# A graph network on one core: where the fourth quarter of the edge distances is made, and how often groups of VectorE instructions signal

## The chip, the cores and the metric

The kernel runs on one core of a Trainium2 chip. The metric is the device time of one execution in microseconds (us). TensorE (PE) multiplies matrices, VectorE (DVE) does elementwise work, reductions and scans, ScalarE (ACT) evaluates functions, GpSimd (POOL) issues the indirect transfers, and SyncE (SP) the others. The engines run their own instruction streams and wait for each other by semaphores.

## What is computed

A graph has 12,500 nodes of 64 features and 212,500 edges. Four layers follow one another, each added to its input and normalised. Cut to what matters (`seg` sums the rows of one node):

```python
# layer 0, twice:  out = D_inv * seg(e[edge_idx], node_idx);  e = B_inv * seg(xt[node_idx], edge_idx)
# layer 1:         softmax of edge_attr_64 @ W_fcr.T over each dst, applied to (h[src] + eh)
# layer 2, similarity:
Wr, Wc = Wh[row], Wh[col]
sim = sum(Wr * Wc) / maximum(|Wr| * |Wc|, EPS)
prop = seg((base * relu(+-sim))[:, None] * Wc, row)
# layer 3:
d = gelu(layer_norm(edge_attr_3 @ Wd1 + bd1, g1, b1))
d = gelu(layer_norm(d @ Wd2 + bd2, g2, b2))            # the edge distances
logits = w1[dst] - w2[src] + d
a = softmax of logits over each dst
out = seg(a * (w3[src] + d), dst)
```

The distances `d` need only the edge attributes, not the nodes, so they may be made in any earlier stage. They are used in the last one.

## The kernel before, in words

**Tiling.** The edges are padded to 128 x 1664: each of the 128 partitions holds 1664 edges in a row (`NT`). A pass takes `T` = 64 columns of edges at a time, so it has 26 chunks (`NCH`) of 8192 edges. The softmax passes take 52 columns and have 32 chunks.

**A pass over the edges.** The helper `gathers` issues 64 indirect transfers per chunk from POOL (L923), one for each column, which fetch a row of a node table for every edge into `rows[b]`, b = 0 or 1. When a chunk is there, DVE runs one `tensor_tensor_scan` for each of the 64 features over the chunk's columns, which makes the running sums of each node, and copies the last column as the start of the next chunk. SP loads the indices `idx` of a chunk and stores its sums.

**The stages**, in order: `sum_pass("conv0d")`, `sort_edges`, `moved_pass`, `sum_pass("conv1d")`, `sum_pass("conv1s")`, `softmax_pass("L1")`, `similarity_pass`, `softmax_pass("L3")`, with small phases between them. The first sum stage over sums is meant by conv1d, the second by conv1s. Each is a block of its own; engines meet between blocks.

**The distances** are made by the class `Distances` in parts of 16 columns. A part is two halves. For half 0, PE transposes the attributes (L981) and multiplies (L986), ACT copies and squares (L1015, L1017), DVE reduces and scales (L1046, L1047), ACT takes the root, DVE divides and applies gain and offset (L1050, L1051, L1054 twice), and ACT applies Gelu. Half 1 does the same on Gelu's result, after PE's transposes and multiplications (L997, L1002, L1004) and ACT's copies (L1024, L1026). There is one buffer `Y`, so the parts follow one another. SP loads the attributes (L971) and stores the part, 512 KB (L976). 26 parts are a quarter of all. conv0d makes quarter 0, conv1d quarter 1, both with one part in each chunk (`per` = 1), and conv1s makes quarters 2 and 3 with two parts in each chunk (`per` = 2).

In a chunk of a sum stage DVE does half 0 of the first part, the 64 scans, the copy, half 1, and with `per` = 2 then both halves of the second part. In conv1d the sums are also multiplied by a share (`mean`, L1235). SP's order is that of `load`, `step` and `store` at L1150 to L1175: load the indices of chunk n, store chunk n-1 (sums and distances), load those of chunk n+1, and so on. POOL starts a chunk's gathers when its indices are there and the store of the sums two chunks back has landed.

**The similarity stage** has no distances, and PE and ACT do nothing in it. In a chunk DVE runs 65 scans over `own` (L2029: the row of the edge's own node, spread over its edges), a copy (L2031), then a chain of eleven instructions (L2041 to L2051) that computes the similarity and multiplies the gathered rows, and 64 scans over the result `tmp` (L2054) with a copy (L2056). The end of L2051 is the signal `msg`; POOL starts the gathers of a chunk when `msg` of the chunk two before has come.

Every one of these scans adds one to a semaphore, and the instruction behind the group waits for the full count:

```python
                    for f in range(F):
                        dve.tensor_tensor_scan(rows[b][:, :, f], k, rows[b][:, :, f], last[:, f:f + 1],
                                               ALU.mult, ALU.add).then_inc(scanned, 1)
                    dve.wait_ge(scanned, (ch + 1) * F)
```

`keep_p` holds, for each edge, whether its node goes on from the column before. In the sum stages it lies as 16-bit numbers in the PSUM tile `held`, in the similarity stage as f32 in a PSUM tile of its own.

Of the kernel before, what the change touches and what calls it, by code (L numbers as in the profile page):

```python
# [32 lines left out]
def gnn_resnorm(nc, x_in, src_0, dst_0, attr3_0, attr64_0, w_0, w2_0, W, out):  # L33
# [239 lines left out]
    class Counting:  # L273
# [38 lines left out]
        def dve(self, dve, i, b):  # L312
            for k in range(T // KC):
# [3 lines left out]
                for d, oh in self.oh[k % 2].items():  # L317
# [3 lines left out]
                    dve.tensor_tensor(oh[:, :, :], v, u, ALU.is_equal).then_inc(self.ready, 1)  # L321
# [6 lines left out]
        def pe(self, pe, i, b):  # L328
            for k in range(T // KC):
                n = (i * 2 + b) * (T // KC) + k  # L330
                pe.wait_ge(self.ready, (n + 1) * 4)
# [124 lines left out]
    def sort_edges(first_row, key, second, third, fill=False):  # L456
# [13 lines left out]
        with ExitStack() as c, nc.Block() as block:  # L470
# [145 lines left out]
            def _(dve):  # L616
# [6 lines left out]
                def digits(i, b):  # L623
                    ch = i * 2 + b
                    dve.wait_ge(loaded[b], (i + 1) * 48)
                    if not zero(i):
                        dve.wait_ge(ohr, ch * 2 * NGP - 2 * NGP)
# [7 lines left out]
                def onehots(ch, b, g):  # L635
                    for src, dst, w in ((lo[b], ohl, P), (hi[b], ohh, HI)):
                        v = src[:, 4 * g:4 * g + 4].unsqueeze(2).to_broadcast([P, 4, w])
                        u = iota[:, 0:w].unsqueeze(1).to_broadcast([P, 4, w])
                        dve.tensor_tensor(dst[b][:, 4 * g:4 * g + 4, :], v, u, ALU.is_equal).then_inc(ohr, 1)
# [47 lines left out]
                def fill_part(i, b, g):  # L687
# [8 lines left out]
                    if g >= GF:  # L696
                        n = NGP - GF
                        for f in range((F + 1) * (g - GF) // n, (F + 1) * (g - GF + 1) // n):
                            v = ec[:, ::-1] if f == F else recs[b][:, ::-1, f]
                            dve.tensor_tensor_scan(recs[b][:, ::-1, f], nxp[:, ::-1], v, after[:, f:f + 1],  # L700
                                                   ALU.mult, ALU.add).then_inc(tail, 1)
                    if g == NGP - 1:
                        dve.wait_ge(tail, (ch + 1) * (F + 1))
# [20 lines left out]
            def _(pe):  # L724
# [4 lines left out]
                def turn(ch, g, b):  # L729
                    if not (zero(ch) and g < 2):  # L730
                        pe.wait_ge(tev, ch * NGP + g - 1)
                    pe.wait_ge(ohr, (ch * NGP + g + 1) * 2)
# [390 lines left out]
    def sum_pass(name, o, idx_arr, table, to, last, first, per, mean=False, hist=None, beside=()):  # L1123
# [6 lines left out]
        with ExitStack() as c, nc.Block() as block:  # L1130
# [18 lines left out]
            def _(sp):  # L1149
# [16 lines left out]
                def store(i, b):  # L1166
# [5 lines left out]
                    else:  # L1172
                        sp.wait_ge(scanned, (i * 2 + b + 1) * F)
# [39 lines left out]
            def _(dve):  # L1213
# [3 lines left out]
                def scan(i, b):  # L1217
# [37 lines left out]
    def moved_pass(last):  # L1255
# [11 lines left out]
        with ExitStack() as c, nc.Block() as block:  # L1267
# [71 lines left out]
            def _(dve):  # L1339
# [3 lines left out]
                for n in range(NM):  # L1343
# [17 lines left out]
                    for f in range(F):  # L1361
                        dve.tensor_tensor_scan(rows[b][:, 0:w, f], kc, rows[b][:, 0:w, f], last[:, f:f + 1],
                                               ALU.mult, ALU.add).then_inc(scanned, 1)
                    dve.wait_ge(scanned, (n + 1) * F)
# [23 lines left out]
    def softmax_pass(name, idx_arr, table, last, lastmax):  # L1388
# [16 lines left out]
        with ExitStack() as c, nc.Block() as block:  # L1405
# [21 lines left out]
            def _(sp):  # L1427
# [29 lines left out]
                def store(ch):  # L1457
                    sp.wait_ge(maxed, ch + 1)
                    sp.dma_start(cols(maxes, ch, TS), Hh[:, 0:TS, :]).then_inc(mstored, 16)
                    sp.wait_ge(summed, (ch + 1) * 2 * F)  # L1460
# [46 lines left out]
            def _(act):  # L1507
# [9 lines left out]
                def fades(i, b):  # L1517
                    ch = i * 2 + b
                    act.wait_ge(dk, ch + 1)
                    if not (isinstance(i, int) and i == 0 and b == 0):  # L1520
                        act.wait_ge(summed, ch * 2 * F)
# [34 lines left out]
            def _(dve):  # L1556
# [3 lines left out]
                def step(i, b):  # L1560
# [19 lines left out]
                    for f in range(F):  # L1580
                        dve.tensor_tensor_scan(Hh[:, 1:TS + 1, f], l[:, :, f], k, Hh[:, 0, f:f + 1],  # L1581
                                               ALU.max, ALU.add).then_inc(hs, 1)
                    dve.wait_ge(hs, (ch + 1) * F)
# [636 lines left out]
```

## Time and profile before

| | us |
|---|---|
| median of 3 runs (lowest, highest) | 24007.1 (23978.64, 24059.23) |
| the profiled execution | 24218.6 |
| its span | 24216.7 |
| DVE busy | 11770.1 (49%) |
| POOL busy | 11836.6 (49%) |
| PE, ACT busy | 4210.8 (17%), 3105.3 (13%) |
| conv1d, from its first gather to its last | 2463 |
| conv1s, the same | 3150 |
| similarity, the same | 2701 |

The profile takes one execution; busy times are sums over all instructions of an engine, and the stages' times are stretches of the span. POOL and DVE are each busy for half of the span, PE and ACT much less. No engine is near its full time, so the order in which engines wait for one another in a chunk has to be read from the trace. The granted TensorE clock was 0.551 of full speed on average.

### The profile page before, as it was taken

How to read it: one execution, taken by the hardware profiler on the slowest of the kernel's cores; microseconds unless marked ns; L12 is line 12 of the kernel's file. 1: busy time of each engine (PE TensorE's matmuls, PEld its weight loads, DVE VectorE, ACT ScalarE, POOL GpSimd, SP SyncE). 2: the span in 40 equal slices, each digit the busy share in tenths (PEclk: the TensorE clock that was granted, in tenths of full speed). 3: DMA queues.
4: the chain of work that ended last, by engine and by line, in shares of the span. 5: the costliest groups of instructions: out<-in, count | busy, mean ns of one | idle time of the engine just before them, and what ended most of it. 6: DMA issues, size and time to landing. Idle time of an engine off the chain costs nothing. (4 is left out here: it accounts for less than half of the span.)

```text
span 24216.7 us, 113497 instructions
## 1 busy us (share of the span) xinstructions
PE 4210.8 (17%) x22758; PEld 3202.0 (13%) x22758; DVE 11770.1 (49%) x32045; ACT 3105.3 (13%) x3839; POOL 11836.6 (49%) x12292
## 2 busy tenths in 40 slices
PE   1222224444440111112222211111100000000000
PEld 1111123333330100001111111111100000000000
DVE  4544554444446233333333346666644454566666
ACT  0101111111110111112222211111100000111111
POOL 5444434333332666654444455555465555545444
PEclk7555557666665555555555555555555555555555
DMA  2111111111114111111111122222222221222222
GB/s 60 38 34 39 38 49 44 44 44 44 44 40 204 41 52 49 52 45 43 43 44 40 44 69 83 84 83 85 76 59 55 63 62 54 89 96 98 99 97 83
DMA packets 546330, 1518.63 MB, mean 63 GB/s; under 512 B 263864, under 2 KB 264397, under 8 KB 494082
## 3 DMA queue, kind: packets, MB, share of 16 engines
q1 hardware_dynamic: 151550, 1028.87, 11.1%
q0 software_dynamic: 392160, 467.91, 9.5%
q10 hardware_dynamic: 2068, 16.12, 0.2%
q14 instruction: 404, 3.31, 0.0%
q8 instruction: 148, 2.42, 0.0%
HBM read 714.46 MB, written 803.57 MB: 63 GB/s over the span
## 5 line engine op out<-in xcount | busy, mean ns | idle before, releaser
L923 POOL DMA_INDIRECT rows<-tab,idx x6656 | 6420.4, 965 | 5273.0 <-issue 2073.0
L571 POOL DMA_INDIRECT moved_rows<-recs,sidx x1664 | 1623.4, 976 | 2362.4 <-DVE sidx L685 1863.6
L1226 DVE TENSOR_TENSOR_SCAN rows<-held,last,rows 128x64 f32<-128x64 f32 (+1 forms) x4992 | 1421.4, 337 | 2055.6 <-issue 1902.7
L923 POOL DMA_INDIRECT rows<-in_x,idx x1664 | 1591.8, 957 | 1691.0 <-DMA idx<-src_d 1191.2
L923 POOL DMA_INDIRECT rows<-sums,idx x1664 | 1573.8, 946 | 1580.1 <-DMA idx<-sedge 1080.3
L1609 DVE TENSOR_TENSOR_SCAN DN<-XB,last,VB 128x52 f32<-128x52 f32 x4096 | 1062.1, 313 | 1261.8 <-issue 1261.4
L1609 DVE TENSOR_TENSOR_SCAN DN<-XB,last,PB 128x52 f32<-128x52 f32 x4096 | 957.4, 307 | 555.4 <-issue 432.7
L2029 DVE TENSOR_TENSOR_SCAN own<-keep_p,lastu,own 128x64 f32<-128x64 f32 x1690 | 543.9, 345 | 1198.7 <-issue 1188.3
L654 DVE CUSTOM_DVE_ANT_0 junk<-pV,ohh 128x98 f32<-128x98 f32 x1664 | 425.5, 256 | 1377.2 <-remote 1137.5
L321 DVE TENSOR_TENSOR oh_dl<-dig_dl,held 128x2048 bf16<-128x2048 uint16 (+1 forms) x104 | 237.7, 2286 | 1485.5 <-remote 1143.0
L986 PE MATMUL dist_ps<-dist_w,a3T 65*128 65x512 f32 x416 | 392.8, 1100 | 3259.8 <-ACT a3T L1010 2347.3
L1581 DVE TENSOR_TENSOR_SCAN H<-logits,H,neg_d 128x52 f32<-128x52 f32 x4096 | 901.5, 304 | 84.9 <-issue 84.9
L1046 DVE TENSOR_REDUCE held<-SQ 128x16 f32<-128x1024 f32 x208 | 254.9, 1225 | 1221.2 <-ACT SQ L1017 769.5
L646 DVE TENSOR_TENSOR same<-pE,mask 128x384 bf16<-128x384 f32 x832 | 440.9, 554 | 770.8 <-remote 509.3
L755 PE MATMUL pV<-place,ohT 128*128 128x98 f32 x1664 | 389.8, 320 | 1947.8 <-issue 927.2
L1485 PE MATMUL pt<-ident,side 128*128 128x128 f32 x832 | 219.8, 412 | 2713.6 <-issue 1491.9
L743 PE MATMUL pE<-ohT 128*128 128x256 f32 x1664 | 633.7, 468 | 229.4 <-issue 179.7
L335 PE MATMUL H_d<-oh_dl,oh_dh 128*98 128x128 bf16 x1664 | 387.7, 305 | 1490.7 <-issue 1013.7
L1640 PE MATMUL pT<-ident,lastmax 128*64 128x128 f32 x2 | 0.8, 393 | 3536.5 <-PEq L62 3536.5
L608 ACT ACTIVATE place<-pP 128x98 f32<-128x98 f32 x832 | 210.7, 253 | 3000.9 <-remote 1354.4
L986 PEld LDWEIGHTS dist_ps<-dist_w,a3T 65*128 65x128 f32 x416 | 122.2, 324 | 3402.1 <-issue 3334.2
L755 PEld LDWEIGHTS pV<-place,ohT 128*128 128x128 f32 x1664 | 284.4, 214 | 2036.2 <-issue 1603.5
(416 smaller groups left out, 16622.0 us busy)
## 6 DMA issues: line engine op xcount, KB each, us to landing
sums<-DN SPq DMA_DIRECT2D x64, 3328.0 KB
sums<-rows SPq DMA_DIRECT2D x52, 2048.0 KB
rows<-tab,idx POOLq DMA_INDIRECT x6656
maxes<-H SPq DMA_DIRECT2D x64, 1664.0 KB
spread<-zeros SPq DMA_DIRECT2D x52, 1040.0 KB
own<-spread SPq DMA_DIRECT2D x26, 2080.0 KB
dists<-Y SPq DMA_DIRECT2D x104, 512.0 KB
recs<-sums SPq DMA_DIRECT2D x26, 2048.0 KB, 16.2
```

Source lines behind the costliest of these rows:

```text
L335: last = pe.matmul(self.H[o][0:HI, :], oh[o + "h"][:, t, :], oh[o + "l"][:, t, :], start=False, stop=False, skip_group_check=True)
L571: pool.indirect_dma_start(moved_rows if fill else rec, bass.IndirectOffsetOnAxis(ap=idx[b][:, j:j + 1], axis=0), recs[b][:, j, :], None).t ...
L646: dve.tensor_tensor(same[g % 2][h][:, :, :], pE[h][:, :, :], mask[:, :, :], ALU.mult).then_inc(msk, 1)
L654: dve.tensor_tensor_reduce(out=junk[:, :], in0=pV[h][:, k, 0:HI], in1=ohh[b][:, t, :], scale=1.0, scalar=0.0, op0=ALU.mult, op1=ALU.add, a ...
L743: pe.matmul(pE[h][:, 0:2, :].rearrange("p a e -> p (a e)"), o[:, 2 * h, :], o[:, 2 * h:2 * h + 2, :].rearrange("p a e -> p (a e)"), start= ...
L755: pe.matmul(pV[h][:, 0, 0:HI], o[:, 2 * h, :], place[:, :], start=True, stop=False)
L923: pool.indirect_dma_start(rows[b][:, j, :], None, table, bass.IndirectOffsetOnAxis(ap=idx[b][:, j:j + 1], axis=0)).then_inc(rows_in[b], 16)
L986: t = pe.matmul(self.p1[:, 8 * h:8 * h + 8, :].rearrange("p a f -> p (a f)"), self.a3T[:, :], dist_w[:, h * 512:(h + 1) * 512], start=True ...
L1226: dve.tensor_tensor_scan(rows[b][:, :, f], k, rows[b][:, :, f], last[:, f:f + 1], ALU.mult, ALU.add).then_inc(scanned, 1)
L1581: dve.tensor_tensor_scan(Hh[:, 1:TS + 1, f], l[:, :, f], k, Hh[:, 0, f:f + 1], ALU.max, ALU.add).then_inc(hs, 1)
L1609: dve.tensor_tensor_scan(DN[:, :, s_ * F + f], XB[:, :, f], a[:, f, :], last[:, s_ * F + f:s_ * F + f + 1], ALU.mult, ALU.add).then_inc(su ...
L2029: dve.tensor_tensor_scan(u[:, :, f], k, u[:, :, f], lastu[:, f:f + 1], ALU.mult, ALU.add).then_inc(filled, 1)
```

## The change

1. conv1s is called with `per` = 1 in place of 2, so it makes only quarter 2.
2. Quarter 3 is made in `similarity_pass`: it gets a `Distances` with one part in each chunk, an instruction stream for PE and one for ACT, half 0 ahead of DVE's step and half 1 behind it, and the load and store on SP. To make room, `keep_p` becomes 16-bit numbers in the tile `held`, and the small tile `a` moves into it too.
3. Groups signal once: in a group of scans, and in the groups that make one-hot masks, only the last instruction adds to the semaphore, and the waits' counts are divided accordingly. That takes out about 23,600 signals: 4914 in the three sum stages, 882 in `moved_pass`, 8128 and 4032 in the softmax passes (L1609, L1581), 3302 in the similarity stage, 1664 in `sort_edges`, and some 700 of the one-hot masks.

The diff, cut to its core (the groups that are not shown are changed in the same way):

```diff
@@ sum_pass, SP and DVE
-                        sp.wait_ge(scanned, (i * 2 + b + 1) * F)
+                        sp.wait_ge(scanned, i * 2 + b + 1)
...
                     for f in range(F):
-                        dve.tensor_tensor_scan(rows[b][:, :, f], k, rows[b][:, :, f], last[:, f:f + 1],
-                                               ALU.mult, ALU.add).then_inc(scanned, 1)
-                    dve.wait_ge(scanned, (ch + 1) * F)
+                        t = dve.tensor_tensor_scan(rows[b][:, :, f], k, rows[b][:, :, f], last[:, f:f + 1],
+                                                   ALU.mult, ALU.add)
+                    t.then_inc(scanned, 1)
+                    dve.wait_ge(scanned, ch + 1)
@@ similarity_pass
-            a, keep_p, keep_in = ps(c, "a", [P, T]), ps(c, "keep_p", [P, NT]), sem("L2_keep_in")
+            held, pa, gains = ps(c, "held", [P, 1024], I32), ps(c, "pa", [P, P]), ps(c, "gains", [P, 4, F])
+            keep_p, keep_b, keep_in = held[:, 0:NT // 2].bitcast(U16), alloc(c, "keep_b", [P, NT], U16), sem("L2_keep_in")
+            a, ss = held[:, 896:896 + T].bitcast(F32), held[:, 960:960 + DW].bitcast(F32)
+            dist = Distances(c, "L2", 3, 1, pa, gains, ss)
@@ similarity_pass, SP
                     sp.dma_start(base[b][:, :], cols(sbase, ch)).then_inc(side_in[b], 16)
+                    dist.load(sp, i, b, 0)
                     if not isinstance(i, int) or i or b:
-                        store(ch - 1)
-
-                def store(ch):
-                    sp.wait_ge(scanned, (ch + 1) * F)
+                        store(*((i - 1, 1) if b == 0 else (i, 0)))
+
+                def store(i, b):
+                    ch = i * 2 + b
+                    sp.wait_ge(scanned, ch + 1)
                     sp.dma_start(cols(sums_s[0:EP, :], ch), tmp[:, :, :]).then_inc(stored, 16)
+                    dist.store(sp, i, b, 0)
@@ similarity_pass, PE and ACT
+            @block.tensor
+            def _(pe):
+                def step(i, b):
+                    dist.pe_first(pe, i, b, 0)
+                    dist.pe_second(pe, i, b, 0)
+                pairs(pe, step)
+
+            @block.scalar
+            def _(act):
+                pairs(act, lambda i, b: dist.act(act, i, b, 0))
@@ similarity_pass, DVE
                     k = keep_p[:, bass.ds(ch * T, T)]
+                    dist.dve(dve, i, b, 0, 0)
                     dve.wait_ge(side_in[b], (i + 1) * 32)
...
                     dve.tensor_copy(last[:, :], tmp[:, T - 1, :]).then_inc(carried, 1)
+                    dist.dve(dve, i, b, 0, 1)
@@ the calls
-        sum_pass("conv1s", "s", sedge, sums, sums_s, last, 2, 2)
+        sum_pass("conv1s", "s", sedge, sums, sums_s, last, 2, 1)
```

**SP in the loop of conv1s**, the piece ahead of the load of a chunk's indices. Before, two parts are stored and two loads of attributes lie around them:

```order
L976 DMA dists<-Y 128x1024
L1173 ISA
L1174 ISA
L1174 DMA sums_s<-rows_614 128x4096
L975 ISA
L976 ISA
L976 DMA dists<-Y 128x1024
L969 REGISTER_ALU
L971 ISA
L971 DMA a_634<-attr_d 128x48
L1153 ISA
L1153 DMA idx_612<-sedge 128x64
```

The same piece now, with the line numbers of the changed kernel:

```order
L1177 DMA sums_s<-rows_614 128x4096
L978 ISA
L979 ISA
L979 DMA dists<-Y 128x1024
L1156 ISA
L1156 DMA idx_612<-sedge 128x64
```

The indices are now loaded behind one store of distances where there were two.

**DVE in the similarity stage**, between the scans over `tmp` of one chunk and those over `own` of the next. Before:

```order
L2054 SCALAR_TENSOR_TENSOR tmp<-keep_p,last,tmp 128x64 x64
L2056 COPY last<-tmp 128x64
L2029 SCALAR_TENSOR_TENSOR own_827<-keep_p,lastu,own_827 128x64 x65
L2031 COPY lastu<-own_827 128x65
L2041 TENSOR_TENSOR tmp<-own_827,rows_825 128x4096
```

Now:

```order
L2087 COPY last<-tmp 128x64
L1049 TENSOR_REDUCE held<-SQ 128x16
L1050 TENSOR_SCALAR held<-held 128x16
L1053 RECIPROCAL held<-held 128x16
L1054 TENSOR_TENSOR Y<-Y,held 128x1024
L1057 TENSOR_TENSOR Y<-Y,gains 128x1024 x2
L1049 TENSOR_REDUCE held<-SQ 128x16
L1050 TENSOR_SCALAR held<-held 128x16
L1053 RECIPROCAL held<-held 128x16
L1054 TENSOR_TENSOR Y<-Y,held 128x1024
L1057 TENSOR_TENSOR Y<-Y,gains 128x1024 x2
L2058 SCALAR_TENSOR_TENSOR own_827<-held,lastu,own_827 128x64 x65
```

Half 1 of one part and half 0 of the next now stand between the two groups of scans.

**SP in the loop of the similarity stage**, one step. Before:

```order
L1981 ISA
L1982 ISA
L1982 DMA idx_822<-sdst 128x64
L1990 ISA
L1990 DMA own_827<-spread 128x4160
L1991 DMA base_829<-sbase 128x64
L1997 ISA
L1997 DMA sums_s<-tmp 128x4096
```

Now:

```order
L1992 DMA idx_822<-sdst 128x64
L2000 ISA
L2000 DMA own_827<-spread 128x4160
L2001 DMA base_829<-sbase 128x64
L974 ISA
L974 DMA a_856<-attr_d 128x48
L2009 ISA
L2009 DMA sums_s<-tmp 128x4096
L978 ISA
L979 ISA
L979 DMA dists<-Y 128x1024
```

A load of attributes (24 KB) now stands ahead of the store of the sums, and a store of distances (512 KB) behind it.

## Rows read from the trace of the kernel before

**Rows 1.** Windows conv1d, conv1s, similarity: us, busy (x) PE PEld DVE ACT POOL, clock.

```profile
8024.00:10487.00 2463.00, 354.07 (x827) 183.05 (x828) 884.97 (x1977) 331.96 (x401) 1573.75 (x1664) 0.51 0.19 49
10541.00:13691.00 3150.00, 683.05 (x1618) 351.31 (x1618) 1008.43 (x2210) 650.38 (x781) 1573.76 (x1664) 0.51 0.16 42
17638.00:20339.00 2701.00, 0.00 (x0) 0.00 (x0) 1287.33 (x3472) 0.00 (x0) 1578.04 (x1664) 0.50 0.23 60
```

**Rows 2.** Timeline of a chunk of conv1s: start us, us, instruction, idle before.

```profile
12110.72 0.94 POOL L923 DMA_INDIRECT rows<-sums,idx  x1 [41.85 <-DMA idx<-sedge]
...
12122.89 7.12 DVE L1226 TENSOR_TENSOR_SCAN rows<-held,last,rows 128x64 f32<-128x64 f32 x29 [0.45 <-issue]
...
12186.52 0.21 DVE L1229 COPY last<-rows 128x64 f32<-128x64 f32 x1 [8.08 <-DMA moved_rows<-dist_w]
...
12196.31 1.22 DVE L1054 TENSOR_TENSOR Y<-Y,gains 128x1024 f32<-128x1024 f32 x1 [0.18 <-DVE Y L1054]
...
12198.85 0.36 SPq L976 DMA_DIRECT2D dists<-Y  x1
...
12205.01 1.23 DVE L1046 TENSOR_REDUCE held<-SQ 128x16 f32<-128x1024 f32 x1 [7.48 <-ACT SQ L1017]
...
12223.36 1.23 DVE L1046 TENSOR_REDUCE held<-SQ 128x16 f32<-128x1024 f32 x1 [12.58 <-ACT SQ L1029]
...
12226.65 2.47 DVE L1054 TENSOR_TENSOR Y<-Y,gains 128x1024 f32<-128x1024 f32 x2
...
12231.95 0.36 SPq L1153 DMA_DIRECT2D idx<-sedge  x1
...
12234.54 0.95 POOL L923 DMA_INDIRECT rows<-sums,idx  x1 [44.08 <-DMA idx<-sedge]
```

**Rows 3.** Timeline of a chunk of conv1d, from the end of its scans.

```profile
9133.30 0.32 DVE L1229 COPY last<-rows 128x64 f32<-128x64 f32 x1 [8.79 <-DMA moved_rows<-dist_w]
...
9137.58 4.42 DVE L1235 TENSOR_TENSOR rows<-rows,held 128x4096 f32<-128x4096 f32 x1 [3.83 <-issue]
...
9156.12 0.95 POOL L923 DMA_INDIRECT rows<-tab,idx  x1 [7.51 <-issue]
```

**Rows 4.** Timeline of a chunk of the similarity stage, DVE and POOL.

```profile
18024.64 15.58 DVE L2054 TENSOR_TENSOR_SCAN tmp<-keep_p,last,tmp 128x64 f32<-128x64 f32 x64
18025.49 0.95 POOL L923 DMA_INDIRECT rows<-tab,idx  x1 [25.84 <-DVE tmp L2051]
...
18040.25 0.20 DVE L2056 COPY last<-tmp 128x64 f32<-128x64 f32 x1
...
18040.58 4.46 DVE L2029 TENSOR_TENSOR_SCAN own<-keep_p,lastu,own 128x64 f32<-128x64 f32 x18
...
18062.88 0.35 DVE L2029 TENSOR_TENSOR_SCAN own<-keep_p,lastu,own 128x64 f32<-128x64 f32 x1 [1.06 <-issue]
...
18113.99 0.20 DVE L2031 COPY lastu<-own 128x65 f32<-128x65 f32 x1 [5.97 <-remote]
...
18130.77 0.95 POOL L923 DMA_INDIRECT rows<-tab,idx  x1 [25.53 <-DVE tmp L2051]
```

**Rows 5.** Timeline of PE in conv0d while a gather ran; these matmuls signal nothing.

```profile
1613.41 0.26 PE L335 MATMUL H_d<-oh_dl,oh_dh 128*98 128x128 bf16 x1 [2.53 <-issue]
1616.21 0.27 PE L335 MATMUL H_s<-oh_sl,oh_sh 128*98 128x128 bf16 x1 [2.54 <-issue]
```

**Rows 6.** Timeline of L1's softmax pass at a gather's end, then DVE's scans.

```profile
15616.94 0.95 POOL L923 DMA_INDIRECT rows<-tab,idx  x1 [0.30 <-issue]
...
15624.63 0.76 DVE L1609 TENSOR_TENSOR_SCAN DN<-XB,last,VB 128x52 f32<-128x52 f32 x3 [0.37 <-issue]
15625.31 5.95 DVE L1609 TENSOR_TENSOR_SCAN DN<-XB,last,PB 128x52 f32<-128x52 f32 x27
```

**Rows 7.** Timeline of conv1s: a hand-over from PE to ACT while a gather runs.

```profile
12147.17 2.08 PE L1004 MATMUL dist_ps<-bd_d,yT 128*128 128x128 f32 x8
...
12172.52 0.60 ACT L1026 ACTIVATE Y<-dist_ps 128x512 f32<-128x512 f32 x1 [27.41 <-DMA klast<-dst_d]
```

**Rows 8.** Costliest groups, the page's part 5: busy, mean ns | idle before.

```profile
L1581 DVE TENSOR_TENSOR_SCAN H<-logits,H,neg_d 128x52 f32<-128x52 f32 x4096 | 901.5, 304 | 84.9 <-issue 84.9
```

More of the change, by code:

```diff
@@ L330, in pe @@
                 n = (i * 2 + b) * (T // KC) + k
[L331 removed]
+                pe.wait_ge(self.ready, n + 1)
                 for t in range(KC):
@@ L699, in fill_part @@
                             v = ec[:, ::-1] if f == F else recs[b][:, ::-1, f]
-                            dve.tensor_tensor_scan(recs[b][:, ::-1, f], nxp[:, ::-1], v, after[:, f:f + 1],
-                                                   ALU.mult, ALU.add).then_inc(tail, 1)
+                            t = dve.tensor_tensor_scan(recs[b][:, ::-1, f], nxp[:, ::-1], v, after[:, f:f + 1],
+                                                       ALU.mult, ALU.add)
                     if g == NGP - 1:
-                        dve.wait_ge(tail, (ch + 1) * (F + 1))
+                        t.then_inc(tail, 1)
+                        dve.wait_ge(tail, ch + 1)
                         dve.tensor_copy(after[:, :], recs[b][:, 0, 0:F + 1]).then_inc(kept, 1)
@@ L1361, in _ @@
                     for f in range(F):
-                        dve.tensor_tensor_scan(rows[b][:, 0:w, f], kc, rows[b][:, 0:w, f], last[:, f:f + 1],
-                                               ALU.mult, ALU.add).then_inc(scanned, 1)
-                    dve.wait_ge(scanned, (n + 1) * F)
+                        t = dve.tensor_tensor_scan(rows[b][:, 0:w, f], kc, rows[b][:, 0:w, f], last[:, f:f + 1],
+                                                   ALU.mult, ALU.add)
+                    t.then_inc(scanned, 1)
+                    dve.wait_ge(scanned, n + 1)
                     dve.tensor_copy(last[:, 0:F], rows[b][:, w - 1, 0:F]).then_inc(carried, 1)
@@ L2005, in _ @@
                 step(NCH // 2 - 1, 1, last=True)
-                store(NCH - 1)
+                store(NCH // 2 - 1, 1)
                 sp.wait_ge(stored, NCH * 16)
+                sp.wait_ge(dist.stored, NCH * 16)
             @block.gpsimd
@@ L2011, in _ @@
                 gathers(pool, tab65, idx, rows, idx_in, rows_in, lambda e, i, b: e.wait_ge(msg, i * 2 + b - 1), go, T, NCH)
+            @block.tensor
[7 more added lines that the diff above has]
+                pairs(act, lambda i, b: dist.act(act, i, b, 0))
             @block.vector
             def _(dve):
+                dist.start(dve)
                 dve.memset(last[:, :], 0.0).then_inc(carried, 1)
                 dve.memset(lastu[:, :], 0.0).then_inc(carried, 1)
-                dve.tensor_copy(keep_p[:, :], keep["s"][:, :]).then_inc(keep_in, 1)
+                dve.tensor_copy(keep_b[:, :], keep["s"][:, :]).then_inc(keep_in, 1)
                 dve.wait_ge(keep_in, 1)
+                dve.tensor_copy(held[:, 0:NT // 2], keep_b[:, :].bitcast(I32)).then_inc(keep_in, 1)
+                dve.wait_ge(keep_in, 2)
                 NS = 10
```

51 lines of the change are left out of this document (29 added, 22 removed).

## The prediction, written before the changed kernel was timed

> **What bounds the kernel now.** The page's busy shares name no engine, so I went by stage. The windows give, for the same 1664 gathers of POOL, 2463 us in conv1d, 3150 in conv1s and 2701 in the similarity stage [rows 1]. POOL is busy for 1574 in each, and with the 0.30 between two gathers [rows 6] it could do a stage in 1574 + 1664 x 0.30 = 2073. All that is above this is POOL waiting, once a chunk. The timelines show for what.
>
> In conv1s a chunk goes from 12110.72 to 12234.54, 123.8 us. DVE's copy after the scans is at 12186.52, half 1 of the first part ends at 12197.53, then the second part waits 7.48 and 12.58 for ACT and ends at 12229.12. Only then come the indices, and POOL has stood idle for 44.08 [rows 2]. So conv1s is bound by DVE's chain, with the second part bare at its end.
>
> In the similarity stage a chunk goes from 18025.49 to 18130.77, 105.3. POOL issues for 79.8 and waits 25.53 for L2051 [rows 4]. The scans over `tmp` run beside the gathers' start, 64 in 15.58. Of the scans over `own`, 18 go quickly (4.46), and then one takes 0.35 with 1.06 idle ahead of it, 1.4 in all, until the gathers are over. Their copy comes at 18113.99, 8.75 after POOL's last transfer and 88.5 into the chunk. L2041 to L2051 take the last 16.8. So DVE, slowed while POOL gathers, bounds this stage.
>
> **The slowing is the point to understand.** After the gathers' end it is gone: in L1 POOL's last gather begins at 15616.94, and from 15625.31 on 27 scans take 5.95 [rows 6]. Is it the scans' signals? PE in conv0d has matmuls that signal nothing, and beside a gather they too start 2.80 apart, with 2.53 idle ahead of each, 1.40 for each of matmul and weight load [rows 5]. So what is slowed is every instruction's end, with or without a signal. Hand-overs are late as well: PE's L1004 ended at 12149.25, and ACT began L1026 at 12172.52, 23.3 later [rows 7].
>
> **Part 1, conv1s with one part.** Removed in each chunk are both halves of the second part and their two waits: 12229.12 - 12197.53 = 31.6 on the path, as the indices are then loaded behind the first part's store (it was issued at 12198.85) and not the second's. Times 26 this is **-821**, and the stage takes 2329. The nearest stage with one part is conv1d. As it stands it takes 2463, which gives -687. Without its mean (9133.62 to 9142.00, 8.4 a chunk [rows 3], 218 in all) it takes 2245, which gives -905. I take -821, since it is conv1s's own rows, and it lies between. Could the 2 MB store of the sums take the indices' place? In conv1d POOL begins 22.8 after the scans' copy, 8.4 of it the mean [rows 3]. In conv1s it would begin at 12202.95, 16.4 after the copy, so about the same distance.
>
> **Part 2, the quarter in the similarity stage.** On DVE two halves of 5.76 (12223.36 to 12229.12) are added, half 1 behind the scans over `tmp`, half 0 ahead of those over `own`. Between them ACT's Gelu, the store of `Y`, PE's first matmuls, ACT's copy and square must be done, 7.48 in conv1s [rows 2]. The scans over `own` start now at +15.1 (from the chunk's first gather). With nothing late they would start at +15.1 + 5.8 + 7.5 + 5.8 = +34.2. What hides this: the slowed scans, which last until about +85, some five after POOL's last transfer (before, 47 x 1.4 from +19.5 gives the same). 18 quick scans bring it to +38.7, by +85 there are 33 at 1.4, and the 14 left are quick again, 3.5, so the copy is at +88.5, where it was. But this hand-over now lies inside a gather. If PE's signal is late once by 23.3 as in [rows 7], half 0 ends at +57.5, 18 quick scans end at +62, 16 at 1.4 end at +85, and the other 31 take 7.7, which is +92.7, or 4.2 more a chunk. If it comes only with the gathers' end, half 0 ends at +91, 65 quick scans take 16.1, and the copy is at +107, 18.4 more a chunk, +478. Below nothing: the copy has 5.97 idle ahead of it that a late signal ends [rows 4]. With 64 signals fewer this could shrink, -155 at most. I take the one late signal, 4.2 x 26 = **+109**, since [rows 7] is the same kind of hand-over. At the stage's end the last half 1, its Gelu and store are bare, 5.8 + 7.5 = **+13**. The rest is covered: PE's and ACT's work of half 1 has from +57 to +105 and then until +120, where half 1 stands, and it needs 12.58 once the gathers are over. POOL's queue gets nothing. On SP the distances' store waits behind the sums' store for a Gelu. Behind it stand the loads of the next step, and those wait for the next `msg` anyway, some 65 later. The 16-bit `keep_p` in PSUM costs nothing: conv1s's scans read it so, 29 in 7.12, 0.246 each, against 15.58 / 64 = 0.243.
>
> **Part 3, groups signal once.** By [rows 5] an instruction is slowed without a signal too, so the 1.4 us stay and the gain is **0**. The waits behind a group wait for the last scan, as before. The opposite reading is the first rival. The Trainium skill (VectorE: DVE Perf Modes, The DRAIN you can't avoid) says the same of a quiet engine: eight copies took as long with a signal each as with one at the end. It would make part 3 nothing everywhere, and no run here shows that yet.
>
> **Sum.** -821 + 109 + 13 = -699. The profiled execution's 24218.6 would become 23520. The median of the runs is 211.5 lower, and I take the same difference from it: 24007.1 - 699 = **23308**. Its own range is 22950 (-905, -155) to 23600 (-687, with the late signal twice as dear).
>
> **Rivals.**
>
> *The similarity stage takes the halves in full (16%).* The hand-over between half 1 and half 0 waits for the gathers' end in every chunk. For it speaks that PE's signals can be late by more than 23; against it that a gather's first third is mostly not slow yet (the scans over `tmp` and 18 more). -821 + 478 + 13 = -330 gives 23677, and 23811 with -687.
>
> *The signals are what is slow (8%).* Then scans that signal nothing run at 0.245 beside a gather, DVE is done early, and POOL bounds the stages at 2073: conv1d -390, conv1s -1077, similarity -624, together -2091, so 21916, and less with the softmax passes. For it: nearly all of DVE's instructions signal, so its rows alone can't tell. Against it: PE's rows.
>
> *A signal costs a little on a quiet engine (5%).* A 64 wide scan takes 0.243, a 52 wide one 5.95 / 27 = 0.220. This leaves 0.12 that doesn't go with the width, and that could at most be the signal. On the path are 82 quick scans a chunk in the similarity stage (256) and L1581's 4032, which run quickly throughout [rows 8] (484): -740 at most, half of it -370. 24007.1 - 699 - 370 = 22938, at most 22568. The Trainium skill has such a rule for PE (TensorE: Matmul & The Clock Gate, The cost: per-tile semaphore tail): increments serialise, some 26 ns each. If it held here for all 23,600, the estimate from that page would be 620 less, 22687.
>
> *Slower: half 1 waits out the gathers (4%).* If the chain PE, ACT, PE, ACT between half 0 and half 1 isn't done by +120, half 1 falls into the next gather. When it comes only after the scans' present end, +88.5, then half 1, the hand-over, half 0, 65 quick scans and L2041 to L2051 follow one by one: 88.5 + 5.8 + 7.5 + 5.8 + 16.1 + 16.8 = 140.5 a chunk in place of 105.3, +915. With -821 and +13 it is +107, 24114. It decides from 31.6 us a chunk on, what conv1s gives back. Against it: POOL stands still for 25 us ahead of +105, and PE and ACT are quick then (12.58 for the whole chain). Something between this and the rival above, about even, gets 3%.
>
> *conv1s keeps its time (2%).* The store of the sums would have to end as late as the second part did. Then only part 2 is left, +122, 24129.
>
> **Chances and range.** The forecast has 62%, the rivals 16, 8, 5, 4 and 2, about even 3. A measurement of this kernel tells 0.3% (72 us) from no change. Faster by more: 62 + 16 + 8 + 5 = 91%, within 3%, slower 4 + 2 = 6%. The range from 22900 to 23820 takes in the forecast's own, the full price in the similarity stage and the middle of the small signals, and leaves out some 17%.
>
> **What would show it.** conv1s's window is near 2329, with one store of distances ahead of the indices and POOL's idle time at a chunk's start near 12 in place of 44. The similarity window is near 2823, half 0 ends at about +57 and the copy L2061 is at +93. Scans without a signal are still 1.4 apart beside a gather, in every stage, and conv1d stays at 2463 within 1%. I am wrong if conv1d or the softmax passes become shorter (the signals), if half 0 stands at the gathers' end (the full price), or if half 1 does (slower).

## The result and the profile after

The changed kernel takes 23137.8 us (median of 4, 23132.6 to 23152.7) against 24015.5 for the kernel before in the same comparison (4 runs, 23978.6 to 24059.2): ratio 0.9635, 95% interval 0.9618 to 0.9652, 878 us less. Forecast were 23308 and 699 less, with a range of 22900 to 23820.

One thing has to be known to understand the numbers below: this kernel takes quite different times on different chips. On two of the chips that the experiments fell on it takes 16950, on two others 24016 and 24234, and what differs in the traces is whether instructions are held up while POOL gathers. Ratios are therefore always against the kernel before on the same chip.

The stages, from the first gather of each to its last, from the two profiles:

| | before | after | |
|---|---|---|---|
| conv1d | 2463 | 2425 | -38 |
| conv1s | 3150 | 2360 | -790 |
| conv1s's last gather to the next gather | 127 | 44 | -83 |
| similarity | 2701 | 2751 | +50 |
| similarity's last gather to the next | 104 | 130 | +26 |
| first softmax pass | 3160 | 3078 | -82 |
| second softmax pass | 3267 | 3146 | -121 |
| profiled execution | 24218.6 | 23132.6 | -1086 |

The profiled execution of before was 203 above the median of its runs, and above the longest of them (24059.2). That of after was 5 below. So the -1086 of the two profiles is 208 too large. Before's profile has the stages that this kernel has on the chip where it takes 24234 (`f1_softmax_signals` below), so it probably comes from a chip of that kind and not from that of the comparison; the record doesn't name its chip. Small differences between stages that the change hardly touches (conv1d, the softmax passes) can't be trusted for this reason.

The windows of the changed kernel, for conv1d, conv1s and the similarity stage, which answer to [rows 1]:

```profile
7990.00:10415.00 2425.00, 356.95 (x830) 183.82 (x830) 881.76 (x1976) 333.11 (x403) 1573.76 (x1664) 0.50 0.19 50
10465.00:12825.00 2360.00, 356.91 (x830) 183.78 (x830) 766.04 (x1926) 333.10 (x402) 1573.87 (x1664) 0.50 0.19 52
16600.00:19351.00 2751.00, 353.42 (x826) 182.65 (x826) 1518.91 (x3756) 325.18 (x393) 1577.50 (x1664) 0.50 0.23 64
```

PE's and ACT's work has moved: half of it is gone from conv1s, and as much stands in the similarity stage. POOL's 1574 is unchanged.

The timeline of a chunk's end in conv1s, which answers to [rows 2]:

```profile
11270.72 0.20 DVE L1233 COPY last<-rows 128x64 f32<-128x64 f32 x1 [9.46 <-DMA moved_rows<-dist_w]
...
11279.12 2.48 DVE L1057 TENSOR_TENSOR Y<-Y,gains 128x1024 f32<-128x1024 f32 x2 [0.88 <-DVE Y L1054]
...
11289.08 1.23 DVE L1049 TENSOR_REDUCE held<-SQ 128x16 f32<-128x1024 f32 x1 [7.48 <-ACT SQ L1020]
```

SP and POOL there:

```profile
11282.94 0.36 SPq L979 DMA_DIRECT2D dists<-Y  x1
11283.49 0.35 SPq L1156 DMA_DIRECT2D idx<-sedge  x1
...
11286.56 0.94 POOL L926 DMA_INDIRECT rows<-sums,idx  x1 [22.50 <-DMA idx<-sedge]
```

Half 1 ends at 11281.6, one store of distances goes out, the indices follow, and POOL starts 5.0 after half 1's end. Its wait is 22.50 where it was 44.08, and in every second chunk it doesn't wait at all (the chunks are 80.0 and 102.4 long in turn, 91.2 in the mean).

A chunk of the similarity stage, DVE and then POOL, which answers to [rows 4]:

```profile
18078.93 15.58 DVE L2084 TENSOR_TENSOR_SCAN tmp<-held,last,tmp 128x64 f32<-128x64 f32 x64
...
18094.65 1.22 DVE L1049 TENSOR_REDUCE held<-SQ 128x16 f32<-128x1024 f32 x1
...
18107.89 1.23 DVE L1049 TENSOR_REDUCE held<-SQ 128x16 f32<-128x1024 f32 x1 [7.48 <-ACT SQ L1020]
...
18114.00 4.70 DVE L2058 TENSOR_TENSOR_SCAN own<-held,lastu,own 128x64 f32<-128x64 f32 x19 [0.35 <-issue]
...
18132.28 0.35 DVE L2058 TENSOR_TENSOR_SCAN own<-held,lastu,own 128x64 f32<-128x64 f32 x1 [1.04 <-issue]
...
18169.39 1.80 DVE L2058 TENSOR_TENSOR_SCAN own<-held,lastu,own 128x64 f32<-128x64 f32 x7 [0.36 <-issue]
18171.23 0.20 DVE L2061 COPY lastu<-own 128x65 f32<-128x65 f32 x1
```

```profile
18079.77 0.95 POOL L926 DMA_INDIRECT rows<-tab,idx  x1 [28.14 <-DVE tmp L2081]
...
18188.01 0.94 POOL L926 DMA_INDIRECT rows<-tab,idx  x1 [28.48 <-DVE tmp L2081]
```

The hand-over between half 1 and half 0 takes 7.48, as in conv1s, though it now lies inside a gather. It did so in every chunk from the fourth on (7.33 in the third). The scans over `own` begin 19.1 later in the chunk than before (+34.2 against +15.1), the scans that signal nothing are still 1.4 apart, and the copy is at +91.5 against +88.5. The 5.97 that ended with a late signal ahead of the copy are gone. A chunk is 108.2 long, where it was 105.3 to 106.8.

### The profile page after: what moved, and what is told of

Same layout as the page of the kernel before. It is cut to its first block and busy times, and to the rows that moved or that the text cites. A ratio compares the mean times of both kernels' runs of the same rounds, so it can differ in the third digit from the quotient of the medians.

```text
span 23130.7 us, 113218 instructions
## 1 busy us (share of the span) xinstructions
PE 4197.8 (18%) x22758; PEld 3187.2 (14%) x22758; DVE 11747.5 (51%) x32052; ACT 3103.9 (13%) x3839; POOL 11833.6 (51%) x12292
## 5 line engine op out<-in xcount | busy, mean ns | idle before, releaser
L1229 DVE TENSOR_TENSOR_SCAN rows<-held,last,rows 128x64 f32<-128x64 f32 (+1 forms) x4992 | 1428.5, 338 | 2062.6 <-issue 1911.5
L2058 DVE TENSOR_TENSOR_SCAN own<-held,lastu,own 128x64 f32<-128x64 f32 (+1 forms) x1690 | 518.0, 341 | 932.9 <-issue 927.1
L1586 DVE TENSOR_TENSOR_SCAN H<-logits,H,neg_d 128x52 f32<-128x52 f32 x4096 | 901.5, 305 | 85.2 <-issue 85.2
L1005 PE MATMUL dist_ps<-dist_b,ones_row 1*128 1x512 f32 x416 | 388.6, 1030 | 1177.2 <-issue 1121.8
```

Source lines behind the costliest of these rows:

```text
L1005: pe.matmul(self.p2[:, :, :].rearrange("p a f -> p (a f)"), ones_row[:, :], dist_b2[:, :], start=True, stop=False)
L1229: t = dve.tensor_tensor_scan(rows[b][:, :, f], k, rows[b][:, :, f], last[:, f:f + 1], ALU.mult, ALU.add)
L1586: t = dve.tensor_tensor_scan(Hh[:, 1:TS + 1, f], l[:, :, f], k, Hh[:, 0, f:f + 1], ALU.max, ALU.add)
L2058: t = dve.tensor_tensor_scan(u[:, :, f], k, u[:, :, f], lastu[:, f:f + 1], ALU.mult, ALU.add)
```

## The experiments

Twelve runs were made, in four groups; two of them repeat a kernel. The first seven fell on two chips without the slowing.

### Which part of the change is worth what

`e1_signals_only` is the kernel before with groups that signal once. `e2_move_only` is the changed kernel with a signal from each instruction. In `e3_no_fourth_quarter` (from before) and `e4_after_no_halves` (from after) the fourth quarter isn't made, and zeros are stored in its place:

```diff
# e2_move_only, in each group
-                        t = dve.tensor_tensor_scan(...)
-                    t.then_inc(scanned, 1)
-                    dve.wait_ge(scanned, ch + 1)
+                        dve.tensor_tensor_scan(...).then_inc(scanned, 1)
+                    dve.wait_ge(scanned, (ch + 1) * F)
# e3_no_fourth_quarter; e4_after_no_halves stores the same zeros and has no Distances in similarity_pass
-        sum_pass("conv1s", "s", sedge, sums, sums_s, last, 2, 2)
+        sum_pass("conv1s", "s", sedge, sums, sums_s, last, 2, 1)
+                    sp.dma_start(cols(dists, ch, DW, 3 * QUARTER), zero[:, :, :]).then_inc(zst, 16)
```

Expected of `e1_signals_only`:

> The kernel before with groups that signal once, and nothing else. Theory A (signals are free, the whole gain is the chain taken from the second sum stage): 24015, within 0.3%, every stage as before. Theory B (the 180 us by which the change beat the sum are the signals): 23800 to 23870, with conv1d at about 2424 in place of 2462, L1 at 3078 in place of 3160 and L3 at 3146 in place of 3267, as in the changed kernel. Theory C (the profiled execution of before was a long one in the softmax passes, chance): as A in the median.

Of `e2_move_only`:

> The changed kernel with a signal from every instruction again. A: 23140, within 0.3% of the changed kernel. B: 23320, with conv1d at 2462 and L1 and L3 back at 3160 and 3267. By the trace the scans over own that slow down beside a gather should be 1.4 us apart in both.

Of `e3_no_fourth_quarter`:

> The kernel before with one part per chunk in conv1s; the fourth quarter of the distances isn't made, zeros are stored in its place from the similarity stage, by 26 stores of the same size. It gives the worth of the second part in conv1s. A: conv1s 2350 in place of 3149 and its tail 80 shorter, the similarity stage as before, so 24015 - 880 = 23135. If the gain were not all in conv1s, it would be above 23250.

Of `e4_after_no_halves`:

> The changed kernel without the fourth quarter's work in the similarity stage (zeros are stored in its place). It gives the price of the quarter there. By the stages of the two profiles (2750 against 2700, and the tail 26 longer) 23138 - 76 = 23060. If signals matter (B) it lies 180 below e3_no_fourth_quarter, if they don't (A) at the same time as that.

Measured, with the kernel before at 16949.8 (15 runs): 16876.2 (ratio 0.9956, 0.9943 to 0.9970), 16939.7 (0.9994, 0.9985 to 1.0003), 16850.3 (0.9942, 0.9929 to 0.9956) and 16841.6 (0.9936, 0.9923 to 0.9950). None of the times expected came out, since all of them were for a chip with the slowing. To have the changed kernel itself beside these, it was run next, with `r2_signals_only` (the same kernel as `e1_signals_only`) and a placement test:

> The changed kernel itself, since the first four runs fell on a chip where the kernel before takes 16950 and no scan beside a gather is 1.4 us from the next. On such a chip: conv1s is bound by POOL at 80.0 a chunk with one part or with two (both profiles show 80.0), so the move is worth nothing and only the signals are left: 16870, ratio 0.995. On a chip that takes 24015 for the kernel before: ratio 0.963 as in the first comparison.

> Groups signal once and nothing else. On a chip without the slowing: 0.9956 again. On one with it: A (signals are free beside a gather) 1.000 within 0.003, so the whole of the changed kernel's 0.037 is the move. B (signals account for what my sum missed) 0.992 to 0.994.

The test `r3_half0_behind_own`:

```diff
-                    dist.dve(dve, i, b, 0, 0)
                     dve.wait_ge(side_in[b], (i + 1) * 32)
...
                     dve.tensor_copy(lastu[:, :], u[:, T - 1, :]).then_inc(carried, 1)
+                    dist.dve(dve, i, b, 0, 0)
                     dve.wait_ge(rows_in[b], (i + 1) * 16 * T)
```

> The changed kernel with half 0 placed behind the scans over own instead of ahead of them. If the slowing of the scans until some 9 us behind the gather's end is what hid half 0 (theory A), half 0 is now bare: 5.8 a chunk more, less the 2 that it costs now, +100 us against the changed kernel (23240 where the kernel before takes 24015). If half 0 cost its time ahead of the scans too, the two are equal. On a chip without the slowing, DVE is done with time to spare and the two are equal too.

Measured on another chip, also without the slowing, with before at 16950.1: the changed kernel 16844.9 (0.9938, 0.9922 to 0.9955), signals only 16876.3 (0.9957, 0.9940 to 0.9974), half 0 behind the scans 16842.4 (0.9937, 0.9921 to 0.9954). Here the whole change is worth 105 us, not 878. Signals only came out as expected, and half 0's place made no difference, as expected of such a chip. The changed kernel was expected at 16870, the move being worth nothing, and took 25 less. The windows of `r2_signals_only` (two parts in conv1s) show why, conv1s, the similarity stage and the second softmax pass:

```profile
7123.00:9201.00 2078.00, 707.89 (x1669) 363.76 (x1670) 931.75 (x2232) 672.70 (x808) 1569.94 (x1664) 0.51 0.24 65
11997.00:14153.00 2156.00, 0.00 (x0) 0.00 (x0) 1199.19 (x3617) 0.00 (x0) 1647.79 (x1664) 0.50 0.28 76
14359.00:16572.00 2213.00, 0.00 (x0) 0.00 (x0) 1961.97 (x6127) 484.13 (x211) 1669.33 (x1664) 0.50 0.42 144
```

and those of `e2_move_only` (one part in conv1s, the other in the similarity stage):

```profile
7136.00:9217.00 2081.00, 353.30 (x858) 182.33 (x858) 665.38 (x1933) 342.56 (x413) 1572.67 (x1664) 0.51 0.22 58
11978.00:14138.00 2160.00, 362.14 (x858) 185.43 (x858) 1470.25 (x3924) 341.31 (x412) 1651.93 (x1664) 0.50 0.30 83
14346.00:16644.00 2298.00, 0.00 (x0) 0.00 (x0) 1956.57 (x6125) 484.15 (x211) 1675.75 (x1664) 0.50 0.40 138
```

conv1s is 2078 with two parts and 2081 with one, both POOL's own 80.0 a chunk. DVE's scans take 15.6 for all 64 inside the gather, and then DVE waits for the transfers, as two rows of `r2_signals_only` in conv1s show:

```profile
8050.85 1.23 DVE L1049 TENSOR_REDUCE held<-SQ 128x16 f32<-128x1024 f32 x1 [12.58 <-ACT SQ L1032]
...
8083.43 15.58 DVE L1229 TENSOR_TENSOR_SCAN rows<-held,last,rows 128x64 f32<-128x64 f32 x64 [9.02 <-DMA rows<-sums,idx]
```

With 9.02 to spare, a part more or less moves nothing within the stage. Behind its last gather it does: from there to POOL's next instruction (L1722) POOL waits 61.62 in `r2_signals_only` and 27.95 in `r1_after`,

```profile
9261.75 0.15 POOL L1722 MEMSET row<- 128x64 f32 x1 [61.62 <-ACTq L1633]
```

```profile
9240.31 0.15 POOL L1722 MEMSET row<- 128x64 f32 x1 [27.95 <-ACTq L1633]
```

so one part more there costs 33.7, about the 31 us by which the changed kernel is below signals only. With the slowing, then, what the move gains within the stage (790) is the price of a chain behind slowed scans.

### The chain, tied to the gathers by a wait

To test that on any chip, the four kernels of the next group make the tie by hand: DVE waits, ahead of the copy behind a chunk's scans, for the gathers in flight. (The last chunk has no such wait.)

```diff
# m1_before_tied, m2_after_tied: in conv1s and in the similarity stage
                     dve.wait_ge(filled, ch + 1)
+                    if not end:
+                        dve.wait_ge(rows_in[1 - b], (i + 1 + b) * 16 * T)
                     dve.tensor_copy(lastu[:, :], u[:, T - 1, :]).then_inc(carried, 1)
# m3_tied_half0_behind: and half 0 behind this copy
# m4_tied_ahead_half0: in the similarity stage the wait stands here instead
+                    if not end:
+                        dve.wait_ge(rows_in[1 - b], (i + 1 + b) * 16 * T)
                     dist.dve(dve, i, b, 0, 0)
```

> On the chip of the first comparison DVE's scans end only with the gathers that run beside them. Here that tie is made by a wait: in conv1s and in the similarity stage, DVE waits ahead of the copy behind the chunk's scans (over own in the similarity stage) for the gathers that are in flight. This is the kernel before with the tie. Theory A (what the second part costs is its chain behind the gathers' end): conv1s 122.9 a chunk (79.8 + 5.8 + 31.6 + 5.4), similarity 97 (79.8 + 16.8), together 26 x (42.9 + 14) more than 16950, 18430. If the second part could hide elsewhere (rival), conv1s would stay near 91.

> The changed kernel with the same tie. A: conv1s 91.3 a chunk, 31.6 less than m1_before_tied, similarity 97 again, as half 1, its hand-over and half 0 lie beside the gather; together 17500, so the move is worth some 930 with the tie and 0 without. Rival, the halves are paid in the similarity stage also: its chunks 10 to 19 longer than in m1_before_tied, 17800 to 18000.

> m2_after_tied with half 0 behind the scans over own and behind the tied wait's copy. A: half 0 is bare, 5.8 a chunk in the similarity stage, 17650. Without the tie this placement cost nothing (16842 against 16845).

> The changed kernel with the tied wait of the similarity stage ahead of half 0 instead of ahead of the copy: this is the rival with 16%, a hand-over to half 0 that comes only with the gathers' end. By its sum half 0, 65 scans and the chain follow the gathers: 79.8 + 5.8 + 16.1 + 16.8 = 118.5 a chunk, 21 more than m2_after_tied, 18060 in all. If it were less, the rival's price (478) was too high.

These fell on a chip with the slowing (before 24015.5, 13 runs), so the times expected don't apply, and what can be compared is chunks and differences. Measured: 24018.5 (ratio 1.000, 0.9990 to 1.0009), 23236.3 (0.9671, 0.9655 to 0.9687), 23315.6 (0.9708, 0.9691 to 0.9724), 23528.5 (0.9797, 0.9781 to 0.9813). The windows: `m1_before_tied`, conv1s and similarity,

```profile
10492.00:13656.00 3164.00, 682.97 (x1618) 351.16 (x1618) 1005.25 (x2207) 650.20 (x781) 1569.99 (x1664) 0.51 0.15 42
17597.00:20290.00 2693.00, 0.00 (x0) 0.00 (x0) 1273.23 (x3473) 0.00 (x0) 1569.86 (x1664) 0.50 0.23 61
```

`m2_after_tied`, the same two,

```profile
10467.00:12848.00 2381.00, 353.16 (x826) 182.52 (x826) 733.58 (x1919) 329.20 (x397) 1569.99 (x1664) 0.51 0.19 51
16709.00:19466.00 2757.00, 353.44 (x826) 182.62 (x826) 1512.13 (x3754) 324.98 (x393) 1569.98 (x1664) 0.50 0.23 64
```

and the similarity stage of `m3_tied_half0_behind`

```profile
16686.00:19535.00 2849.00, 336.87 (x797) 173.15 (x797) 1523.92 (x3756) 320.78 (x387) 1573.77 (x1664) 0.50 0.23 62
```

and of `m4_tied_ahead_half0`.

```profile
16696.00:19745.00 3049.00, 330.96 (x797) 170.01 (x797) 1388.48 (x3697) 320.71 (x387) 1573.68 (x1664) 0.50 0.21 58
```

Four things follow.

- The tie costs the kernel before nothing (1.000). So on this kind of chip DVE's scans do end with the gathers beside them or later, which is what the reading of the timelines said.
- With the tie a step from chunk to chunk of conv1s is 123.3 with two parts (expected 122.9) and 92.0 with one (91.3), in the mean of 25. The first step is 79.9 in both, since POOL doesn't wait there. In the other 24 the means are 125.1 and 92.5, and the difference, 32.6, is the second part's chain, expected as 31.6. The trace of `m1_before_tied` has that chain at 31.6 in nine chunks and at 33.5 in 17, 32.8 in the mean.
- Half 0 behind the scans costs 92 in the stage's window and 79 in the median over half 0 ahead of them, 3 to 4 a chunk. Expected were 5.8. The two timelines show why it is less: with half 0 behind, the copy comes at +89.7 in place of +91.7, and half 0's 5.8 follow it. That is the sum written for `r3_half0_behind_own`, 5.8 less 2.
- With half 0 held until the gathers' end, the rival with 16%, a chunk is 120.2 (expected 118.5), the stage 292 longer than in `m2_after_tied`, and so is the median (292). The 11.6 a chunk between the two are less than the 21 expected, because `m2_after_tied` has 108.6 and not 97: slowed scans outlast the wait in it. Against `m1_before_tied` the stage is 356 longer, where the rival's price was 478. So that price was too high: half 0 stood at +81.3 and the copy at +103.3, not at +107.

`m2_after_tied` itself is 98 slower than the changed kernel was in the first comparison. 61 of that are in the first softmax pass, where the two kernels have the same code (see the sum below).

Why half 0's place matters so little shows in the timeline of `m4_tied_ahead_half0`:

```profile
18664.55 1.23 DVE L1049 TENSOR_REDUCE held<-SQ 128x16 f32<-128x1024 f32 x1 [60.74 <-DMA rows<-tab,idx]
...
18670.66 15.82 DVE L2073 TENSOR_TENSOR_SCAN own<-held,lastu,own 128x64 f32<-128x64 f32 x65 [0.35 <-DVE Y L1057]
18686.51 0.20 DVE L2076 COPY lastu<-own 128x65 f32<-128x65 f32 x1
```

DVE has stood still for 60.74 of the gathers, starts 1.6 after they end, and runs all 65 scans in 15.82. In the changed kernel, whose DVE was busy beside the gathers, scans are slowed until +89.6, some 10 after POOL's last transfer.

### Where the signals' share lies

```diff
# f1_softmax_signals: the kernel before, with t.then_inc behind the groups of softmax_pass (L1581, L1609) only
-                    dve.wait_ge(summed, (ch + 1) * 2 * F)
+                    t.then_inc(summed, 1)
+                    dve.wait_ge(summed, ch + 1)
```

> The kernel before with groups that signal once in the two softmax passes alone. On the quick chips the second softmax pass took 2297 with a signal per scan (e2_move_only) and 2212 with one per group (e1_signals_only), its scans alike in both (64 in 13.95, 32 in 7.14), and the 85 lie in DVE's wait ahead of L1567's copy (135 against 48 over 14 waits). Theory A (the signals' whole gain is there): 16876 on a quick chip, the same as with all groups changed, ratio 0.9956; on a chip with the slowing 0.996 to 0.998. Theory B (chance of the rhythm between POOL, DVE and the stores, which any edit can tip, as e3_no_fourth_quarter has 2215 with a signal per scan): 16950, or anything between.

It fell on a chip with the slowing: 24203.3 against 24233.8, ratio 0.9986 (0.9977 to 0.9995), 30 us less. That is smaller than the 0.996 to 0.998 of theory A, and more than nothing. 24 of the 30 are in the second softmax pass (3267 in before's profile, 3243 in this one's).

## Why the prediction was right, and where it was off

**The bound.** Right. DVE's chain bounds conv1s and the similarity stage, since slowed scans tie it to the gathers' end. `m1_before_tied` shows the tie itself, and the chips without the slowing show conv1s at POOL's 80.0 a chunk.

**Part 1, -821.** Measured -790 in the window and -83 behind it, -873. The mechanism and the count of 26 parts were right. The mis-sized term is the price of a part, 31.6: it was read from a chunk in which half 1 waits 12.58 for ACT. The trace of before has that wait in eight of the 26 chunks and 14.44 in the other 18, and the second parts last 33.5 in those. All 26 together make 855, 34 more than 821. The other 18 of the 873 aren't assigned. The parts also don't lie where the prediction had them. POOL's first step is 80 with two parts and with one, so the window holds 24 of them (790, or 32.9 each; the tied pair has 32.6), and is 2360 where 2329 was forecast. The other two the kernel before made behind POOL's last gather. Their halves 0 and 1, in the timeline of before:

```profile
13704.83 1.23 DVE L1046 TENSOR_REDUCE held<-SQ 128x16 f32<-128x1024 f32 x1 [7.48 <-ACT SQ L1017]
...
13725.04 1.23 DVE L1046 TENSOR_REDUCE held<-SQ 128x16 f32<-128x1024 f32 x1 [14.44 <-ACT SQ L1029]
...
13776.98 1.23 DVE L1046 TENSOR_REDUCE held<-SQ 128x16 f32<-128x1024 f32 x1 [7.48 <-ACT SQ L1017]
...
13797.19 1.23 DVE L1046 TENSOR_REDUCE held<-SQ 128x16 f32<-128x1024 f32 x1 [14.44 <-ACT SQ L1029]
```

These two cost 33.5 each, 67 of the 83. The chunk of [rows 2] was a short one for the same reason: 123.8, where the steps of before from the third on are 124.9 in the mean. In the changed kernel they are 80.0 and 102.4 in turn.

**Part 2, +109 and +13.** Measured +50 and +26. The step that failed is "the late signal": PE's hand-over would come 23.3 late, as in [rows 7]. It was 7.48 in every chunk from the fourth on. PE's matmul for half 0 falls 21 to 28 into the gather, and [rows 7] was 36 in. The other sum in that paragraph, with nothing late, said half 0 at +28.4, the scans from +34.2 on, and the copy where it was. The first two are exact (+28.1, +34.2), and the copy came 2 to 3 later. There "slowed until +85" was the wrong term: it is +89.6. So the mechanism priced at +109 didn't occur, and the +50 came another way. That a price of this sign and order came out is luck.

What hid most of the delay is a wait that the prediction's sum had left out ("below nothing"). In the chunks from the fourth on, but for the last, the last scan over `own` ended at +85.6 before, in the mean, and the copy behind it started only at +89.4. In the whole stage DVE stood idle for 97.3 us ahead of this copy. Now the last scan ends at +91.4, and that idle time is gone. So the halves push the scans' end back by 5.8 a chunk, 3.8 of it falls into time in which the copy had waited anyway, and 2.0 remain. Fewer signals alone don't end this wait: in `m3_tied_half0_behind`, whose groups signal once and whose scans end at +87.8, the copy still comes at +89.7, long after the gathers' end (+81.3 by the wait in `m4_tied_ahead_half0`). Why it is held until then stays open. The prediction named as cover the scans that are slowed until behind the gathers' end. That covers half 0 only because it lies ahead of them (`m3_tied_half0_behind`). The tail term was low: the last chunk's half 1, Gelu and store, and what follows in the stage, took 26. Here too one chunk was taken for all: 105.3 [rows 4], where most are 106 to 107.

**Part 3, 0.** Right for a scan: its duration and its spacing don't depend on a signal. Beside gathers with the slowing, the page's groups say it for before (L1226) and after (L1229), and for L1581, now L1586, which runs unslowed:

```profile
L1226 DVE TENSOR_TENSOR_SCAN rows<-held,last,rows 128x64 f32<-128x64 f32 (+1 forms) x4992 | 1421.4, 337 | 2055.6 <-issue 1902.7
```

```profile
L1229 DVE TENSOR_TENSOR_SCAN rows<-held,last,rows 128x64 f32<-128x64 f32 (+1 forms) x4992 | 1428.5, 338 | 2062.6 <-issue 1911.5
...
L1586 DVE TENSOR_TENSOR_SCAN H<-logits,H,neg_d 128x52 f32<-128x52 f32 x4096 | 901.5, 305 | 85.2 <-issue 85.2
```

Busy and idle time are the same within 0.5% with 4914 signals fewer, and L1581's 901.5 and 84.9 [rows 8] are now 901.5 and 85.2. So the rival with 8% (an unslowed scan without a signal) and that with 5% (0.12 us a signal) are both excluded. The Trainium skill's sentence on DVE (VectorE: DVE Perf Modes, The DRAIN you can't avoid), that a signal adds nothing, agrees with these rows. Its rule of 26 ns for each increment on PE (TensorE: Matmul & The Clock Gate, The cost: per-tile semaphore tail) doesn't hold for DVE's groups here: 4032 fewer at L1581 would be an estimated 106 us by it, and the rows show 0.

Not borne out for the kernel as a whole: without the slowing, the kernel that signals once took 74 us less (0.44%), and `f1_softmax_signals` took 30 less with it. Where the 74 lie can be seen. The group of DVE's copy at the head of a chunk, in the second softmax pass, `e2_move_only` and `r2_signals_only`:

```profile
L1567 DVE COPY H<-H 128x64 f32<-128x64 f32 x30 | 5.9, 197 | 135.9 <-issue 135.9
```

```profile
L1572 DVE COPY H<-H 128x64 f32<-128x64 f32 x30 | 6.2, 207 | 48.7 <-issue 48.6
```

The copies wait 87 less, and that is all of the 85 by which the pass is shorter. By the program it waits for the store of the running maxima. But `e3_no_fourth_quarter`, with a signal from each scan, has a pass of 2215 too. So it isn't the signals by themselves that set this wait, and what tips it stays open.

**The sum.** -699 forecast, -878 measured. The two large terms that were off, -821 and +109, both made the gain look too small; the +13, too low by 13, took little of that back. From the two profiles come -873 for conv1s with its end and +76 for the similarity stage with its end, -797 together. That leaves 81. The tied pair, both on one chip, differs by 782 between the medians, of which -783 in conv1s, -69 behind it, +64 and +26 in and behind the similarity stage make 762. So there 20 are left, and `f1_softmax_signals`, which has the signals of the softmax passes alone, has 30. The signals' side is thus worth some 20 to 30. The other 50 to 60 are of the size of one difference without a change of code: the first softmax pass, in the changed kernel and then in `m2_after_tied`.

```profile
13026.00:16105.00 3079.00, 487.86 (x2392) 446.41 (x2392) 1916.45 (x5953) 602.47 (x425) 1641.91 (x1664) 0.55 0.26 84
```

```profile
13068.00:16208.00 3140.00, 477.07 (x2380) 439.38 (x2380) 1914.28 (x5931) 601.68 (x424) 1629.27 (x1664) 0.55 0.25 82
```

What makes it 61 shorter in one of them isn't shown. That before's profile probably comes from another kind of chip shows in the same two stages, conv1d and the second softmax pass, of `f1_softmax_signals` (2461 and 3243) and of `m1_before_tied` (2433 and 3208):

```profile
8032.00:10493.00 2461.00, 353.53 (x827) 182.95 (x828) 884.28 (x1976) 331.95 (x401) 1573.30 (x1664) 0.51 0.18 49
20622.00:23865.00 3243.00, 0.00 (x0) 0.00 (x0) 2034.95 (x6043) 484.16 (x211) 1609.26 (x1664) 0.50 0.29 97
```

```profile
8007.00:10440.00 2433.00, 356.23 (x830) 183.77 (x830) 883.22 (x1977) 331.89 (x401) 1569.98 (x1664) 0.51 0.19 50
20564.00:23772.00 3208.00, 0.00 (x0) 0.00 (x0) 2036.08 (x6054) 484.04 (x211) 1609.67 (x1664) 0.50 0.29 98
```

Before has 2463 and 3267. Two sums of the prediction are slightly off, without weight: 2701 - 2073 is 628 and not 624, and the range's upper end by its own terms is 23551 and not 23600.

**The rivals.** The full price in the similarity stage (16%) didn't come: the hand-over wasn't late. `m4_tied_ahead_half0` shows what it would have been, 356 in the stage's window and not 478. Half 1 waiting out the gathers (4%) didn't come either: it stood at +14.9 in every chunk from the fourth on. The 2% case is excluded by conv1s's window.

## What to carry to other kernels

Ask of an engine's work not how long it is but what it ends with. Work that is tied to the end of a transfer has room ahead of it and none behind: the same distances cost about 33 us a chunk behind the gathers and 2 to 3 ahead of them. When pricing such a chain, take it from all chunks and not from one: the one that was read here was among the eight short ones. And the chunks that still run behind the last transfer count too, they were a tenth of the gain here and are what is left of it on a chip without the slowing. And a gain that rests on a disturbance is worth only as much as the disturbance: on chips where the scans aren't slowed, this one is 0.6% and not 3.7%.

## What was not expected of the hardware

- The kernel before takes 16950 us on two chips and 24016 and 24234 on two others. On the first, none of the scans beside a gather is held up. On the others they are 1.4 us apart once a gather has run for a while (from 19 us on in [rows 2], from about 40 on in the changed similarity stage). What differs between the chips isn't visible in the traces.
- In the similarity stage the slowing outlasts the gathers where DVE was busy beside them, by about 10 us in the changed kernel, and not where DVE had stood still (`m4_tied_ahead_half0`: half 0, from 1.6 us behind them on, takes its usual 5.8, and then 65 scans take 15.82). Whether being busy is the reason wasn't tested otherwise.
